# Attention heads of a transformer layer: results normalised in place instead of turned by TensorE, and seven score banks for the last two heads

## The chip, the cores and the metric

The kernel runs on one core of a Trainium2 chip. The metric is the device time of one execution in microseconds (us), the median of several runs. The engines of the core work side by side and wait for each other by semaphores: TensorE (PE; its weight loads are listed as PEld), VectorE (DVE), ScalarE (ACT), GpSimd (POOL) and SyncE (SP), which here issues all the DMAs.

## What is computed

A transformer layer on 4 sequences of 2048 rows of 256: layer norm, self-attention with 16 heads of size 16 and a relative position bias, and a feed-forward part with a router beside it, all added to the input.

```python
def _L0_attn_ref(hidden_states, W_qkv, W_out, rel_emb):      # hidden_states: 4 x 2048 x 256
    qkv = hidden_states @ W_qkv
    ...
    scores = jnp.einsum('bhqd,bhkd->bhqk', q, k)
    scores = scores + compute_bias(rel_emb, S, S)
    attn = jax.nn.softmax(scores.astype(jnp.float32), axis=-1).astype(scores.dtype)
    out = jnp.einsum('bhqk,bhkd->bhqd', attn, v)
    out = jnp.transpose(out, (0, 2, 1, 3)).reshape(B, S, EMBED_DIM)
    return out @ W_out
...
xn = _layernorm(x, axis=-1)
x = x + _L0_attn_ref(xn, ...) + _L0_ffn_ref(xn, ...)
```

## The kernel before

All loops are unrolled, so the order in which instructions are written for each engine is the order in which it takes them. There are three stages.

**Stage 1** (to about 583 us): layer norm, q, k, v, the feed-forward part, the bias, and the row maxima of the first two heads. The change doesn't touch it.

**Stage 2** (to about 3374 us): 64 heads n (4 sequences x 16), each in 16 blocks kb of 128 keys, each block against 2048 queries in four chunks c of 512. For every block TensorE makes four score matmuls (`scores`, L962) into a ring of three PSUM banks, and between them four matmuls for the row maxima of the head two ahead (`maxima`, L946, LEAD = 2) into banks 3 to 6; then the sums of the block two earlier (`sums`, L971, LAG = 2) into bank 7, where the numerators of the head and, in a 17th row of each group of 32, the totals of the softmax gather. ScalarE takes the exponential of each score tile into a buffer prob of four blocks (L832). GpSimd multiplies the parts near the diagonal by the bias factors (L876). VectorE reduces the maxima, two halves a block (L905); TensorE may write the next block's maxima only when it has done so (`wait(pe, max_done, ...)`).

The maxima become the shift of the softmax: at block 8 (TURN_SHIFT) of head n TensorE transposes the maxima of head n+1 (L958), ScalarE copies them to shift_row (L804) and SyncE copies that into a row of the query stack of head n+1 (L775).

The result of head n-1 is finished in head n: at block 2 ScalarE copies bank 7 to o_sb (`collect`, L810); at block 4 (TURN_RESULT) TensorE transposes it with four transposes into a ring bank (L987), ScalarE copies that to o_turned_sb (L816), VectorE takes the reciprocals of the totals (L918), and GpSimd multiplies and writes rows into v_all (`normalise`, L860).

SyncE's order in head n is: load(n+3), the loads of the stacks and bias factors (L144, L770), which wait for head n-1 to be done, then shift(n+1).

**Stage 3** (to the end), 16 chunks of 512 rows: ScalarE packs the results of 16 heads into rows (L1097), TensorE transposes them, ScalarE and VectorE split them in a high and a low part (L1108, L1127), TensorE multiplies by W_out (24 matmuls a chunk, L1171), VectorE adds the base rows (L1139), SyncE stores the chunk and loads base rows for a later one.

Of the kernel before, what the change touches and what calls it, by code (L numbers as in the profile page):

```python
# [14 lines left out]
H, D = 16, 16  # L15
# [28 lines left out]
PROBS = 4  # L44
LAG = 2

# [83 lines left out]
def transformer_layer(nc, x, w_qkv, w_out, rel_emb, router_w, w1, b1, w2, b2, hot, out):  # L130
# [4 lines left out]
    base_d = nc.dram_tensor("base_rows", [B * S, E], F32).ap()  # L135

    def load_stacks(sp, n, q_stack, k_stack, loaded):

        for which, stack, loads in ((0, q_stack, Q_LOADS), (1, k_stack, K_LOADS)):
            for row, part, parts, copies in loads:  # L140
                rows = qk_d[which, part:part + parts, bass.ds(D * n, D), :]
                if copies > 1:
                    rows = rows.to_broadcast([copies, D, S])
                sp.dma_start(stack[D * row:D * (row + parts * copies), :].bitcast(F32), rows).then_inc(loaded, 16)  # L144

    ctx = ExitStack()
    with ctx:
# [21 lines left out]
        with c1:  # L169
# [419 lines left out]
            def _(pe):  # L589
# [22 lines left out]
                def early_scores(b, c, piece):  # L612
# [3 lines left out]
                    for h in range(2):  # L616
                        last = nc.tensor.matmul(ps[:, h], q_early[HALF * h:HALF * h + ROWS, P * i:P * (i + 1)],  # L617
                                                k_early[HALF * h:HALF * h + ROWS, CH * j:CH * (j + 1)], start=True, stop=True)
# [78 lines left out]

        c2 = ExitStack()  # L700
        with c2:
# [3 lines left out]
            ones_row = sb("ones_row", [1, S], F32R, c=c2)  # L705
# [6 lines left out]
            o_sb = sb("o_sb", [P, CH], c=c2)  # L712
            o_turned_sb = sb("o_turned_sb", [P, TPC, CPB, 32], c=c2)
            recip = sb("recip", [P, TPC, CPB], c=c2)

            stacks_in = [sem(f"stacks_in{u}") for u in range(GROUP)]
            shift_in = [sem(f"shift_in{u}") for u in range(GROUP)]
# [3 lines left out]
            v_ones_set = sem("v_ones_set")  # L721
            score_ready = sem("score_ready")
# [6 lines left out]
            shift_turned = sem("shift_turned")  # L729
            o_copied = sem("o_copied")  # L730
            o_turned = sem("o_turned")
            recip_done = sem("recip_done")
            o_done = sem("o_done")

            RING = 3
            MAX_BANK = RING
            SUM_BANK = 7


            TURN_RESULT, TURN_SHIFT = 4, 8  # L740
            RESULT_AT = CPB * TURN_RESULT
            SHIFT_AT = CPB * TURN_SHIFT + 1
            RING_TILES = CPB * KB + 2

            def tile_at(kb, c):

                return CPB * kb + c + (kb >= TURN_RESULT) + (kb >= TURN_SHIFT)

            def drained_at(n, at):


                count = RING_TILES * n + at + 1
                if isinstance(n, int):
                    count += (n == 0 and at < RESULT_AT) - (n == NH - 1 and at >= SHIFT_AT)
                return count
# [8 lines left out]
            def _(sp):  # L764
                def load(n, u):
# [4 lines left out]
                    sp.dma_start(near[u][:], near_d[bass.ds(n % H, 1)].rearrange("a p s c -> (a p) s c")).then_inc(near_in[u], 16)  # L770

                def shift(n, u):

                    wait(sp, drained, 1 if isinstance(n, int) and n == 0 else drained_at(n - 1, SHIFT_AT))
                    sp.dma_start(q_st[u][ROWS:ROWS + 1, :].bitcast(F32).rearrange("a (i p) -> a i p", p=P),  # L775
                                 shift_row[:, n % 2 if isinstance(n, int) else u % 2, :].bitcast(F32)) \
                        .then_inc(shift_in[u], 16)

                def group(g, last=False):
                    for u in range(GROUP):  # L780
                        n = GROUP * g + u
                        if not (last and u > 0):
                            load(n + GROUP - 1, (u + GROUP - 1) % GROUP)
                        if not (last and u == GROUP - 1):
                            shift(n + 1, (u + 1) % GROUP)

                load(0, 0)
                sp.wait_ge(ones_set, 1)
                for u in range(GROUP):
                    sp.dma_start(k_st[u][ROWS:ROWS + 1, :].bitcast(F32), ones_row[:].bitcast(F32)).then_inc(ones_in, 16)  # L790
                shift(0, 0)
                for u in range(1, GROUP - 1):
                    load(u, u)
                group(0)
                for g in range(1, GROUPS - 1):
                    group(g)
                group(GROUPS - 1, last=True)

            @block.scalar
            def _(act):  # L800
                def shift(n, par):

                    wait(act, shift_turned, n + 1)
                    nc.scalar.activation(shift_row[:, par % 2, :], ps[0:KB, SHIFT_AT % RING, 0:P], ACT.Copy).then_inc(drained, 1)  # L804

                def collect(n):

                    wait(act, pv_done, CPB * KB * (n + 1))
                    wait(act, o_turned, n)
                    nc.scalar.activation(o_sb[:], ps[:, SUM_BANK], ACT.Copy).then_inc(o_copied, 1)  # L810

                def collect_turned(n):

                    wait(act, o_turned, n + 1)
                    wait(act, o_done, n)
                    nc.scalar.activation(o_turned_sb[:].rearrange("p i c w -> p (i c w)"), ps[:, RESULT_AT % RING], ACT.Copy) \  # L816
                        .then_inc(drained, 1)

                def head(n, u, first=False, last=False):
                    for kb in range(KB):  # L820
                        if kb == LAG and not first:
                            collect(n - 1)
                        if kb == TURN_RESULT and not first:
                            collect_turned(n - 1)
                        if kb == TURN_SHIFT and not last:
                            shift(n + 1, (u + 1) % GROUP)
                        for c in range(CPB):
                            i = CPB * (KB * n + kb) + c
                            wait(act, score_ready, i + 1)

                            wait(act, pv_done, summed(n, kb - PROBS, c) if kb >= PROBS else summed(n - 1, KB + kb - PROBS, c))
                            nc.scalar.activation(prob[:, kb % PROBS, CH * c:CH * (c + 1)], ps[:, tile_at(kb, c) % RING], ACT.Exp).then_inc(drained, 1)  # L832

                shift(0, 0)
                for u in range(GROUP):
                    head(u, u, first=u == 0)
                for g in range(1, GROUPS - 1):
                    for u in range(GROUP):
                        head(GROUP * g + u, u)
                for u in range(GROUP):  # L840
                    head(NH - GROUP + u, u, last=u == GROUP - 1)
                collect(NH - 1)
                collect_turned(NH - 1)

            @block.gpsimd
            def _(pool):
                def build(n, u, turn):
                    wait(pool, pv_done, CPB * KB * (n - 1))
                    pool.wait_ge(v_ones_set, 2)
                    nc.gpsimd.tensor_copy(vx[:, u % 2, :, 0:D], v_all[:, bass.ds(n, 1)].rearrange("p a k d -> p (a k) d")) \  # L850
                        .then_inc(v_read, 1)

                    pool.wait_ge(near_in[u], 16 * turn)
                    wait(pool, v_read, n + 1)
                    nc.gpsimd.tensor_tensor(vr[:, u % 2], vx[:, u % 2],
                                            near[u][:, 0, 0:1].unsqueeze(2).to_broadcast([P, KB, 32]), ALU.mult).then_inc(v_built, 1)

                def normalise(n):

                    nc.gpsimd.tensor_tensor(  # L860
                        v_all[:, bass.ds(n, 1)].rearrange("p a (c i) d -> p i (a c) d", c=CPB), o_turned_sb[:, :, :, 0:D],
                        recip[:].unsqueeze(3).to_broadcast([P, TPC, CPB, D]), ALU.mult).then_inc(o_done, 1)

                def head(g, u, first=False, last=False):
                    n = GROUP * g + u
                    for kb in range(KB):
                        if kb == TURN_RESULT + 2 and not first:

                            wait(pool, recip_done, n)
                            wait(pool, v_read, n)  # L870
                        if kb == 8 and not last:
                            build(n + 1, (u + 1) % GROUP, g + 1 if u + 1 < GROUP else g + 2)
# [12 lines left out]
                for u in range(GROUP):  # L885
                    head(0, u, first=u == 0)
# [322 lines left out]
```

## Time and profile before

| | |
|---|---|
| median of 3 runs | 3451.89 us (3449.85 to 3497.42) |
| profiled execution | 3448.83 us |
| its span, first to last instruction | 3447.1 us |
| granted TensorE clock, mean | 0.988 of full |
| busy share: PE, DVE, ACT, POOL | 94%, 80%, 72%, 35% |

The profiled execution is one run of the program, 0.1% faster than the median. The span is from the first to the last instruction. A busy share is the time in which an engine works on at least one instruction. In a timeline, each line is an instruction or several like ones: start, duration, engine, line of the kernel, operation, output and inputs, and in brackets the engine's idle time before it with what ended it. Matmuls overlap: each starts before the last has ended. "SPq" is SyncE issuing a DMA; the duration is that of the issue, not of the transfer.

### The profile page before, as it was taken

The numbers are of one execution on the slowest core, as the hardware profiler recorded it, in microseconds if no ns is written. First come the engines' busy times: TensorE is split into PE (matmuls) and PEld (weight loads), VectorE is DVE, ScalarE is ACT, GpSimd is POOL, SyncE is SP. The second block draws the span as 40 slices with busy tenths as digits, with TensorE's granted clock in tenths as the row PEclk, the third lists the DMA queues.
The fourth block names the chain that finished last, engine by engine and source line by source line (L and its number), as shares of the span: only waits on it lengthen the run. The fifth ranks groups of instructions, "written<-read, shape, count | busy, mean of one in ns | idle before, by whom it ended". The sixth has DMA issues, their size and how long they took to land. (4 is left out here: it accounts for less than half of the span.)

```text
span 3447.1 us, 56397 instructions
## 1 busy us (share of the span) xinstructions
PE 3245.1 (94%) x20426; PEld 1573.3 (46%) x20426; DVE 2769.0 (80%) x3046; ACT 2476.0 (72%) x4875; POOL 1203.8 (35%) x1644
## 2 busy tenths in 40 slices
PE   8899997699999999999999999999999999999998
PEld 7788886233333333333333333333333333333337
DVE  5477764588888888888888888888888888888815
ACT  4343443588878887888878888788878887888875
POOL 1112121233433344434444344333443334333430
PEclk9999999799999999999999999999999999999999
DMA  7332323100000000000000000000000000000006
GB/s 183 115 88 74 102 82 101 47 28 28 28 28 28 28 28 28 28 28 28 28 28 28 28 28 28 28 28 28 28 28 28 28 28 28 28 28 28 15 1 199
DMA packets 80480, 156.52 MB, mean 45 GB/s; under 512 B 8088, under 2 KB 48728, under 8 KB 73864
## 3 DMA queue, kind: packets, MB, share of 16 engines
q1 hardware_dynamic: 80200, 152.90, 15.5%
q8 instruction: 161, 2.64, 0.3%
q14 instruction: 119, 0.97, 0.1%
HBM read 101.92 MB, written 56.16 MB: 46 GB/s over the span
## 5 line engine op out<-in xcount | busy, mean ns | idle before, releaser
L905 DVE TENSOR_REDUCE max_half<-ps 128x1 f32<-128x1024 f32 x1984 | 2337.2, 1220 | 337.0 <-PE ps L946 333.6
L832 ACT ACTIVATE prob<-ps 128x512 f32<-128x512 f32 x4096 | 2114.8, 603 | 506.9 <-PE ps L962 506.8
L962 PE MATMUL ps<-q_st,k_st 49*128 49x512 f32 x4096 | 1511.3, 446 | 160.7 <-ACT prob L832 52.5
L946 PE MATMUL ps<-k_st,q_st 48*128 48x512 f32 x3968 | 1569.4, 468 | 0.2 <-DVE max_half L905 0.2
L876 POOL TENSOR_TENSOR prob<-prob,near 128x224 f32<-128x224 f32 (+2 forms) x1408 | 965.1, 691 | 1667.8 <-ACT prob L832 1649.0
L962 PEld LDWEIGHTS ps<-q_st,k_st 49*128 49x128 f32 x4096 | 679.2, 184 | 1334.7 <-ACT prob L832 1142.2
L971 PE MATMUL ps<-prob,vx 128*32 128x512 f32 x4096 | 947.8, 606 | 0.0
L971 PE MATMUL ps<-prob,vr 128*32 128x512 f32 x4096 | 946.1, 604 | 0.0
L946 PEld LDWEIGHTS ps<-k_st,q_st 48*128 48x128 f32 x3968 | 656.3, 184 | 58.7 <-DVE max_half L905 2.5
L608 PE MATMUL ps<-xnt,w_parts 128*128 128x512 f32 x1152 | 276.7, 400 | 16.7 <-DMA k_early<-qk_parts 10.5
L608 PEld LDWEIGHTS ps<-xnt,w_parts 128*128 128x128 f32 x1152 | 218.1, 191 | 70.1 <-DMA k_early<-qk_parts 10.7
L549 ACT ACTIVATE parts<-ps 128x512 fp32r<-128x512 f32 x64 | 38.1, 598 | 272.0 <-PE ps L608 232.6
L971 PEld LDWEIGHTS ps<-prob,vr 128*32 128x32 f32 x4096 | 133.1, 108 | 172.9 <-ACT prob L832 144.9
L673 PE MATMUL ps<-w_parts,hid 128*128 128x256 f32 x1536 | 196.7, 284 | 0.0
L673 PEld LDWEIGHTS ps<-w_parts,hid 128*128 128x128 f32 x1536 | 184.2, 189 | 11.7 <-issue 11.7
L971 PEld LDWEIGHTS ps<-prob,vx 128*32 128x32 f32 x4096 | 132.5, 108 | 78.7 <-ACT prob L832 53.2
L360 POOL TENSOR_TENSOR top_exp<-euler,top_less 128x32 f32<-128x32 f32 x16 | 86.8, 5428 | 160.7 <-DVE top_less L413 160.7
L354 POOL TENSOR_TENSOR rstd<-var_eps,power 128x4 f32<-128x4 f32 x17 | 23.1, 1359 | 307.6 <-DVE var_eps L388 307.6
L557 ACT ACTIVATE hid_raw<-ps,b_sb 128x512 f32<-128x512 f32 x128 | 88.2, 690 | 42.3 <-PE ps L608 32.6
L458 DVE TENSOR_TENSOR parts<-ps,parts 128x512 fp32r<-128x512 f32 x64 | 44.1, 692 | 71.6 <-ACT parts L549 71.6
L475 DVE TENSOR_TENSOR hid<-hid_raw,hid 128x512 fp32r<-128x512 f32 x128 | 85.4, 688 | 19.3 <-ACT hid L564 17.9
L448 DVE TENSOR_REDUCE max_early<-ps 128x2 f32<-128x1024 f32 x64 | 78.4, 1225 | 19.2 <-PE ps L617 18.9
(70 smaller groups left out, 1060.4 us busy)
## 6 DMA issues: line engine op xcount, KB each, us to landing
qk_parts<-parts SPq DMA_DIRECT2D x64, 512.0 KB, 4.6
near<-bias_near SPq DMA_DIRECT2D x64, 352.0 KB, 13.4
q_st<-qk_parts SPq DMA_DIRECT2D x64, 256.0 KB
k_st<-qk_parts SPq DMA_DIRECT2D x64, 256.0 KB
x_sb<-in_L_attn_hidden_states SPq DMA_DIRECT2D x18, 512.0 KB, 6.1
base_rows<-x_sb SPq DMA_DIRECT2D x16, 512.0 KB, 2.9
q_st<-qk_parts SPq DMA_DIRECT2D x64, 128.0 KB
k_st<-qk_parts SPq DMA_DIRECT2D x64, 128.0 KB
```

What stands on the lines that cost most here:

```text
L360: nc.gpsimd.tensor_tensor(top_exp[:], euler[:], top_less[:], ALU.pow).then_inc(exp_done, 1)
L448: nc.vector.tensor_reduce(max_early[:, :, bass.ds(i, 1), j], ps[:, 0:2].unsqueeze(2), AX.X, ALU.max).then_inc(max_done, 1)
L475: nc.vector.tensor_tensor(hid[:, 1, f], hid_raw[:, f % RAWS], hid[:, 0, f].bitcast(F32), ALU.subtract).then_inc(hid_low, 1)
L557: nc.scalar.activation(hid_raw[:, f % RAWS], ps[:, F1_BANKS[f % 4]], ACT.Gelu_apprx_tanh, bias=b1_sb[:, f:f + 1]) \
L608: last = nc.tensor.matmul(to, stationary(a, k), moving(b, k), start=k == 0 and (a, b) == PASSES[0], stop=k == blocks - 1 and (a, b) == PAS ...
L673: last = nc.tensor.matmul(ps[:, F2_BANKS[t % 2], E * (t // 2):E * (t // 2 + 1)], hid[:, a, f, P * t:P * (t + 1)], weight(W_2, b_, f), star ...
L832: nc.scalar.activation(prob[:, kb % PROBS, CH * c:CH * (c + 1)], ps[:, tile_at(kb, c) % RING], ACT.Exp).then_inc(drained, 1)
L876: nc.gpsimd.tensor_tensor(prob[:, kb % PROBS, q0:q1], prob[:, kb % PROBS, q0:q1], near[u][:, side, c0:c0 + q1 - q0], ALU.mult).then_inc(ne ...
L905: nc.vector.reduce_max(max_half[:, par % 2, i, half:half + 1], ps[:, MAX_BANK + 2 * half:MAX_BANK + 2 + 2 * half].rearrange("p a n -> p (a ...
L946: mm = nc.tensor.matmul(ps[:, MAX_BANK + c], q_st[u][0:ROWS, P * i:P * (i + 1)], k_st[u][0:ROWS, CH * c:CH * (c + 1)], start=True, stop=True)
L962: nc.tensor.matmul(ps[:, tile_at(kb, c) % RING], k_st[u][:, P * kb:P * (kb + 1)], q_st[u][:, CH * c:CH * (c + 1)], start=True, stop=True). ...
L971: nc.tensor.matmul(ps[32 * c:32 * (c + 1), SUM_BANK], v[:, u % 2, kb], prob[:, kb % PROBS, CH * c:CH * (c + 1)], start=kb == 0, stop=kb == ...
```

## The change

- The result of a head is no longer turned. It stays in o_sb (now two buffers), transposed as bank 7 has it. SyncE copies the totals from it to total_sb by four DMAs (`totals`), VectorE takes the reciprocals (`reciprocals`, after block TOTAL_AT = 6), SyncE stores them to DRAM and spreads them over recip_rows by four broadcasts (`spread`), GpSimd multiplies o_sb in place (`normalise`, after block NORM_AT = 10), and SyncE copies the result by four DMAs into attn (`keep`), which lies in a new buffer for the first sequence and in v_all for the others. In each head this comes behind shift(n+1) in SyncE's order.
- The shift is turned by TensorE as before, at block TURN_AT = 8.
- prob has three blocks, not four.
- Heads 62 and 63, which have no maxima to make, use seven banks for scores: from tile ALONE on.
- The last stage joins the same block. attn is transposed already, so nothing is packed or turned: ScalarE makes the high part of a chunk (`high`, 128x1024), GpSimd the low part (`low`, 128x1024), TensorE multiplies, VectorE adds. Two chunks are prepared ahead of the last head's end, the others behind it. W_out and the first base rows are loaded in head 1.

```diff
-PROBS = 4
+PROBS = 3
 LAG = 2
+TURNED = 3
...
+            TOTAL_AT, NORM_AT, TURN_AT = 6, 10, 8
+            def tile_at(n, kb, c):
+                return CPB * (KB * n + kb) + c + n + 1 + (kb >= TURN_AT and n < NH - 1)
+            def turn_at(m):
+                return CPB * (KB * (m - 1) + TURN_AT) + m if m > 0 else 0
+            ALONE = tile_at(NH - LEAD, 0, 0)
+            def bank_of(at):
+                return at % RING if at < ALONE else (at - ALONE) % SUM_BANK
...
             @block.sync
+                def shift(n):
+                    wait(sp, drained, turn_at(n) + 1)
+                    sp.dma_start(q_st[n % GROUP][ROWS:ROWS + 1, :]..., shift_row[:, n % 2].bitcast(F32)).then_inc(shift_in[n % GROUP], 16)
+                def totals(n):
+                    sp.wait_ge(o_copied, n + 1)
+                    wait(sp, recip_done, n)
+                    for c in range(CPB):
+                        sp.dma_start(total_sb[32 * c:32 * (c + 1)], o_sb[32 * c + D:32 * c + D + 1, n % 2].rearrange("a (g i) -> a g i", i=PIECE)) \
+                            .then_inc(total_in, 16)
+                def spread(n):
+                    sp.wait_ge(recip_done, n + 1)
+                    sp.dma_start(recip_d[n].rearrange("(p i) -> p i", i=PIECE), recip[:]).then_inc(recip_stored, 16)
+                    sp.wait_ge(recip_stored, 16 * (n + 1))
+                    wait(sp, o_done, n)
...
+                    for c in range(CPB):
+                        sp.dma_start(recip_rows[32 * c:32 * c + D], recip_d[n:n + 1, CH * c:CH * (c + 1)].to_broadcast([D, CH])).then_inc(recip_in, 16)
+                def keep(n):
+                    sp.wait_ge(o_done, n + 1)
...
+                for n in range(NH):
+                    if n + GROUP - 1 < NH:
+                        load(n + GROUP - 1)
+                    if n + 1 < NH:
+                        shift(n + 1)
+                    if n > 0:
+                        totals(n - 1)
+                        spread(n - 1)
+                        keep(n - 1)
...
             @block.scalar
+                for i in range(TURNED - 1):
+                    high(i)
+                collect(NH - 1)
+                for i in range(TURNED - 1, B * CPB):
+                    high(i)
             @block.gpsimd
+                def normalise(n):
+                    pool.wait_ge(recip_in, 16 * CPB * (n + 1))
+                    nc.gpsimd.tensor_tensor(o_sb[:, n % 2], o_sb[:, n % 2], recip_rows[:], ALU.mult).then_inc(o_done, 1)
...
+                for i in range(TURNED - 1):
+                    low(i)
+                normalise(NH - 1)
+                for i in range(TURNED - 1, B * CPB):
+                    low(i)
             @block.vector
+                def reciprocals(n):
+                    dve.wait_ge(total_in, 16 * CPB * (n + 1))
+                    wait(dve, recip_stored, 16 * n)
+                    nc.vector.reciprocal(recip[:], total_sb[:]).then_inc(recip_done, 1)
...
+                for n in range(NH):
+                    for kb in range(KB):
+                        if n + LEAD < NH:
+                            maxima(n + LEAD, kb)
+                        if kb == TOTAL_AT and n > 0:
+                            reciprocals(n - 1)
+                    if n + LEAD < NH:
+                        combine(n + LEAD, max_half)
...
             @block.tensor
-                def turn_result(n):
-                    wait(pe, o_copied, n + 1)
-                    for i in range(TPC):
-                        last = nc.tensor.transpose(ps[:, RESULT_AT % RING, P * i:P * (i + 1)], o_sb[:, P * i:P * (i + 1)], ident[:])
-                    last.then_inc(o_turned, 1)
...
+                        if kb == TURN_AT and n + 1 < NH:
+                            turn(n + 1)
+                        for c in range(CPB):
+                            scores(n, kb, c)
+                            if m < NH:
+                                maxima(m, kb, c)
```

## Rows read from the trace of the kernel before

**Rows 1.** The page's costliest groups: busy, mean ns of one, idle before
```profile
L905 DVE TENSOR_REDUCE max_half<-ps 128x1 f32<-128x1024 f32 x1984 | 2337.2, 1220 | 337.0 <-PE ps L946 333.6
...
L962 PEld LDWEIGHTS ps<-q_st,k_st 49*128 49x128 f32 x4096 | 679.2, 184 | 1334.7 <-ACT prob L832 1142.2
```
**Rows 2.** Timeline of one undisturbed block: start us, duration us, engine
```profile
2028.43 0.50 PE L962 MATMUL ps<-q_st,k_st 49*128 49x512 f32 x1
...
2029.23 2.35 DVE L905 TENSOR_REDUCE max_half<-ps 128x1 f32<-128x1024 f32 x2 [0.26 <-PE ps L946]
...
2029.61 0.50 PE L962 MATMUL ps<-q_st,k_st 49*128 49x512 f32 x1
...
2031.04 0.50 PE L962 MATMUL ps<-q_st,k_st 49*128 49x512 f32 x1
```
**Rows 3.** Timeline around block 8, where the shift is turned
```profile
2021.19 2.36 DVE L905 TENSOR_REDUCE max_half<-ps 128x1 f32<-128x1024 f32 x2 [0.26 <-PE ps L946]
...
2023.21 0.49 PE L962 MATMUL ps<-q_st,k_st 49*128 49x512 f32 x1
...
2023.59 1.04 POOL L855 TENSOR_TENSOR vr<-vx,near 128x512 f32<-128x512 f32 x1
2023.61 0.56 SPq L775 DMA_DIRECT2D q_st<-shift_row  x1
...
2025.82 0.49 PE L962 MATMUL ps<-q_st,k_st 49*128 49x512 f32 x1
```
**Rows 4.** Timeline of SyncE's issues, and DMA issues: KB each, us to landing
```profile
2000.41 1.09 SPq L144 DMA_DIRECT2D q_st<-qk_parts  x2
2001.54 1.17 SPq L144 DMA_DIRECT2D k_st<-qk_parts  x2
...
q_st<-shift_row SPq DMA_DIRECT2D x64, 8.0 KB, 1.8
...
k_st<-ones_row SPq DMA_DIRECT2D x4, 8.0 KB, 3.0
```
**Rows 5.** Timeline around block 4, where the result is turned
```profile
2009.30 0.50 PE L962 MATMUL ps<-q_st,k_st 49*128 49x512 f32 x1
...
2012.50 0.50 PE L962 MATMUL ps<-q_st,k_st 49*128 49x512 f32 x1
...
2015.57 0.24 DVE L918 RECIPROCAL recip<-o_turned_sb 128x16 f32<-128x16 f32 x1
```
**Rows 6.** Stretches: us, busy (instructions) per engine, PEclk, DMA share, GB/s
```profile
583.00:584.00 1.00, 0.10 (x1) 0.00 (x0) 0.96 (x3) 0.00 (x0) 0.00 (x0) 1.00 0.00 0
...
587.00:588.00 1.00, 0.04 (x1) 0.04 (x1) 0.32 (x2) 0.00 (x0) 0.36 (x1) 0.79 0.00 0
...
642.00:643.00 1.00, 1.00 (x10) 0.25 (x10) 1.00 (x2) 1.00 (x3) 0.84 (x2) 0.90 0.15 42
```
**Rows 7.** Timeline of the first head, TensorE at the low clock
```profile
634.90 2.36 DVE L905 TENSOR_REDUCE max_half<-ps 128x1 f32<-128x1024 f32 x2 [0.18 <-PE ps L946]
...
637.32 0.79 PE L946 MATMUL ps<-k_st,q_st 48*128 48x512 f32 x1
...
640.33 0.79 PE L962 MATMUL ps<-q_st,k_st 49*128 49x512 f32 x1
...
643.40 0.50 PE L962 MATMUL ps<-q_st,k_st 49*128 49x512 f32 x1
```
**Rows 8.** Timeline of two blocks of the last head, without maxima
```profile
3355.84 0.96 PE L962 MATMUL ps<-q_st,k_st 49*128 49x512 f32 x3
...
3358.44 0.96 PE L962 MATMUL ps<-q_st,k_st 49*128 49x512 f32 x3
```
**Rows 9.** The last stage: timeline, and one stretch of it
```profile
3373.37 0.60 ACT L810 ACTIVATE o_sb<-ps 128x512 f32<-128x512 f32 x1 [1.94 <-PE ps L971]
...
3392.31 3.11 PE L1171 MATMUL ps<-wo_parts,turned 128*128 128x256 f32 x24
...
3412.00:3416.00 4.00, 4.00 (x36) 4.00 (x35) 2.92 (x7) 2.56 (x7) 0.00 (x0) 1.00 0.88 283
```

More of the change, by code:

```diff
@@ L769, in load @@
                     wait(sp, near_done, NEAR_UP_TO[KB] * (n - GROUP + 1))
[L770 to L787, printed above, removed]
+                    sp.dma_start(near[u][:], near_d[n % H:n % H + 1].rearrange("a p s c -> (a p) s c")).then_inc(near_in[u], 16)
@@ L791, in _ @@
[L791 to L826, printed above, removed]
-                        for c in range(CPB):
[L828 to L843, printed above, removed]
@@ L1072, in batch @@
+                totals(NH - 1)
+                spread(NH - 1)
+                keep(NH - 1)
+                for b in range(B):
                     for c in range(CPB):
-                        wait(sp, res_done, TPC * (CPB * b + c + 1))
-                        sp.dma_start(out[bass.ds(S * b + CH * c, CH), :].rearrange("(t p) e -> p t e", p=P), base_in[:, c]) \
+                        sp.wait_ge(res_done, TPC * (CPB * b + c + 1))
+                        sp.dma_start(out[S * b + CH * c:S * b + CH * (c + 1), :].rearrange("(t p) e -> p t e", p=P), base_in[:, c]) \
@@ new lines, in collect, with head @@
+                def collect(n):
+                    act.wait_ge(pv_done, CPB * KB * (n + 1))
+                    if n > 1:
+                        act.wait_ge(attn_in[(n - 2) // H], 16 * CPB * ((n - 2) % H + 1))
+                    nc.scalar.activation(o_sb[:, n % 2], ps[:, SUM_BANK], ACT.Copy).then_inc(o_copied, 1)
+                def head(n):
+                    for kb in range(KB):
+                        if kb == LAG and n > 0:
+                            collect(n - 1)
+                        if kb == TURN_AT and n + 1 < NH:
+                            shift(n + 1)
+                        for c in range(CPB):
+                            act.wait_ge(score_ready, CPB * (KB * n + kb) + c + 1)
+                            t = KB * n + kb
+                            if t >= PROBS:
+                                act.wait_ge(pv_done, summed((t - PROBS) // KB, (t - PROBS) % KB, c))
+                            nc.scalar.activation(prob[:, t % PROBS, CH * c:CH * (c + 1)], ps[:, bank_of(tile_at(n, kb, c))], ACT.Exp) \
+                                .then_inc(drained, 1)
@@ new lines, in high @@
+                def high(i):
+                    b, c = i // CPB, i % CPB
+                    act.wait_ge(attn_in[b], 16 * CPB * H)
+                    wait(act, proj_ready, TPC * (i - TURNED + 1))
+                    nc.scalar.activation(turned[:, i % TURNED, 0], attn[b][:, :, CH * c:CH * (c + 1)], ACT.Copy).then_inc(a_high, 1)
+                shift(0)
+                for n in range(NH):
+                    head(n)
+                    if n == 2:
+                        act.wait_ge(wo_in, 16)
+                        nc.scalar.activation(wo_parts[:, 0], wo_raw, ACT.Copy).then_inc(wo_high, 1)
@@ L1142, in _, with maxima @@
-                dve.wait_ge(wo_high, 1)
-                nc.vector.tensor_tensor(wo_parts[:, 1], wo_raw[:], wo_parts[:, 0].bitcast(F32), ALU.subtract).then_inc(wo_low, 1)
-                low(0, 0)
-                batch(0)
-                for b in range(1, B - 1):
-                    batch(b)
-                batch(B - 1)
+                def maxima(m, i):
+                    for half in range(2):
+                        dve.wait_ge(max_ready, 2 * (KB * m + i) + half + 1)
+                        if i == 0 and half == 0:
+                            wait(dve, neg_done, m - 1)
+                        nc.vector.reduce_max(max_half[:, m % 2, i, half:half + 1],
+                                             ps[:, MAX_BANK + 2 * half:MAX_BANK + 2 + 2 * half].rearrange("p a n -> p (a n)"), AX.X).then_inc(max_done, 1)
@@ new lines, in sums @@
+                def sums(n, kb):
+                    if kb == 0:
+                        pe.wait_ge(v_built, n + 1)
+                        wait(pe, o_copied, n)
+                    for c in sum_order(kb):
+                        if near_at(kb, c):
+                            pe.wait_ge(near_done, NEAR_UP_TO[KB] * n + near_at(kb, c))
+                        else:
+                            pe.wait_ge(drained, tile_at(n, kb, c) + 1)
+                        v = vr if c < left_chunks(kb) else vx
+                        nc.tensor.matmul(ps[32 * c:32 * (c + 1), SUM_BANK], v[:, n % 2, kb], prob[:, (KB * n + kb) % PROBS, CH * c:CH * (c + 1)],
+                                         start=kb == 0, stop=kb == KB - 1).then_inc(pv_done, 1)
@@ L1156, in turn @@
+                for kb in range(KB - LAG, KB):
+                    sums(NH - 1, kb)
+                pe.wait_ge(wo_low, 1)
+                pe.wait_ge(drained, tile_at(NH - 1, KB - 1, CPB - 1) + 1)
+                for i in range(B * CPB):
+                    pe.wait_ge(a_low, i + 1)
                     for t in range(TPC):
+                        wait(pe, res_done, TPC * (i - 1) + t + 1)
                         for k in range(KE):
-                            last = nc.tensor.transpose(ps[:, TURN_BANKS[c % 2] + k, P * t:P * (t + 1)], rows[:, c % 2, t, P * k:P * (k + 1)],
-                                                       ident[:])
@@ L1178, in _ @@
-                turn(0, 0)
-                turn(1, 1)
-                pe.wait_ge(wo_low, 1)
-                batch(0)
-                for b in range(1, B - 1):
-                    batch(b)
-                batch(B - 1)
+                            for x, y in PASSES:
+                                last = nc.tensor.matmul(ps[:, PROJ_BANK + t, 0:E], turned[:, i % TURNED, x, k, P * t:P * (t + 1)], wo_parts[:, y, k],
+                                                        start=k == 0 and (x, y) == PASSES[0], stop=k == KE - 1 and (x, y) == PASSES[-1])
```

424 lines of the change are left out of this document (156 added, 268 removed).

## The prediction

> **What bounds the kernel now.** I read the table of stretches first, then the costliest groups, then the timeline of single heads. From about 631 to 3373 us the kernel does one thing 64 times: a head of 16 key blocks (kb), 42.8 us each. No engine is full there. The costliest group on VectorE is the row maxima for the head two ahead, 1984 of 1220 ns each; the weight loads of the scores spend most of their idle time behind an exponential [rows 1]. The timeline of one block shows why [rows 2]: the first score starts at 2028.43, the fourth, which needs the ring bank that the first exponential frees, at 2029.61, and the first score of the next block at 2031.04. A block lasts 2.61 us, in this relay between TensorE and ScalarE. VectorE is nearly level with it: its two maxima of the block take 2.35 of those 2.61 us, starting 0.80 us after the first score. So VectorE has 0.26 us of slack a block. TensorE may not write the maxima of block kb+1 before VectorE has read those of block kb (the wait on max_done in maxima). **An instruction that holds VectorE for more than a fraction of a microsecond holds TensorE, and with it everything.** This is what the change has to be read against.
>
> **Part 1: result rows no longer turned.** Before, TensorE turns the summed head at block 4 by four transposes. The block before it, from 2009.30 to the first score behind the transposes at 2012.50, takes 3.20 us in place of 2.61 [rows 2, 5]: 0.59 us, on the path. It goes in heads 1 to 63: 63 x 0.59 = 37 us gained. ScalarE's copy of the turned result goes too; it lay in the wait behind those transposes. The shift's transpose at block 8 stays.
>
> **Part 2: the totals go round by DMA, and where that puts VectorE's wait.** The new order of waits, read from the diff, is this. In head n, VectorE does the maxima of blocks 0 to 6 and then `reciprocals(n-1)` (TOTAL_AT = 6), which waits for `total_in`. The four copies that raise it are issued by SyncE in `totals(n-1)`. SyncE issues them only behind `shift(n+1)`, and that waits for ScalarE's copy of the shift, which TensorE's transpose at block 8 (TURN_AT = 8) releases. So a wait placed after block 6 is satisfied by something that cannot start before block 8. It is no deadlock: TensorE gets through block 7, whose maxima need only those of block 6 read, does the transpose and the first score of block 8, and then stands at the first maximum of block 8, which needs half of block 7's maxima read. Behind it on TensorE stand the other scores and the sums, behind these ScalarE's exponentials and GpSimd's products.
>
> Its size, with t = 0 at the first score of block 8 (2023.21 in the kernel before) [rows 3]. SyncE issues the shift at +0.40. Issues of this kind follow one another by (2001.54 - 2000.41)/2 = 0.57 us [rows 4], so the fourth totals copy starts at 0.40 + 4 x 0.575 = 2.70. The nearest copy by kind and size, shift_row, lands 1.8 us after its issue [rows 4]: 4.50. The reciprocal takes 0.25 [rows 5]: 4.8 with the hand-over. Then two maxima of 1.18 each (half of 2.35) [rows 2]: 5.98 and 7.16. TensorE follows about 0.06 us behind (634.90 + 2.36 = 637.26, and the matmul at 637.32) [rows 7]: at 7.22 it writes the third maximum of block 8. Undisturbed, block 9 would have begun at 2.61.
>
> Meanwhile TensorE has been idle from about 0.5 to 6.0. Does the clock fall? After its last matmul at 583.1 it was granted 1.00 until within the second 587 to 588, where the mean is 0.79, so it fell 4.7 us after it [rows 6]. I take it that 5.5 us of idling is enough: the head goes on at 1.2 GHz and not at 2.4. The cost is in the first head of before, where the loop starts at the low level under the same wait on VectorE [rows 7]: from the matmul at 637.32 (the same third maximum) to the first score of the next block at 640.33 are 3.01 us, and that block, in which the clock rises (0.90 in 642 to 643 [rows 6]), takes 3.07 to 643.40. So block 9 begins at 7.22 + 3.01 = 10.23 and block 10 at 13.30, in place of 5.22. **The delay is 8.1 us a head.** VectorE loses nothing more after that; its halves then end before TensorE asks.
>
> The wait bites where VectorE still has maxima to do, and where there is a head before: n from 1 to 61. 61 x 8.1 = 494 us.
>
> Bounds of this term. If the clock held, the third maximum at 7.22 would be followed by the fourth score at 7.46 and 1.43 us of sums (2029.61 to 2031.04) [rows 2], block 10 would begin at 11.5, and the delay would be 6.3 us: 384 us. If the copies landed like the ones_row copies, at 3.0 [rows 4], it would be 9.3: 567 us. If the clock rose a block later, that block would take about 3.95 (its first-to-fourth score 1.45, then as the 3.01 less the pair, an estimate from [rows 7]) and not 3.07: 9.0, or 549 us. Both together give 10.2.
>
> The skill has a rule against this change here. The Trainium skill, DMA: Bandwidth & Descriptors (Specifications), says that pieces under 512 B are done by read-modify-write, and these copies write 64 B pieces; its section on why small descriptors are slow confines the penalty to HBM, and these go from SBUF to SBUF. By the first the sum would move towards the 3.0 us landing, by the second stay at 1.8. No row of before has pieces of 64 B.
>
> **Part 3: the rest of that round trip.** After the reciprocal SyncE stores it, waits, and issues four broadcasts: 4.8 + 3.0 (landing bound) + 3 x 0.575 + 3.0 puts `recip_in` at about 12.5 after t = 0, while GpSimd asks for it only after the products of block 10, that is after 13.3 + 2. Nothing waits. GpSimd's multiplication, 128x512, costs 1.04 as the nearest such operation does [rows 3]; it lies in GpSimd's idle time. `keep` and its four copies follow at about 17 to 20, long before ScalarE reuses the buffer two heads later, and SyncE is back in time for the loads at the next head. Cover gone: only head 62, whose blocks are short and have no stall. There `recip_in` comes at 12.5, GpSimd's products of block 11 end at about 14.5, and the sums that need them would start at about 12.4: 1 to 2 us once. Taken: +1. Three prob buffers for four cost nothing, since an exponential of kb waits for sums that TensorE has in any case issued before that score.
>
> **Part 4: seven score banks in heads 62 and 63.** Without maxima a block still takes 2.60 us (3355.84 to 3358.44) [rows 8]: the fourth score waits for its ring bank 1.18 us after the first, with three issued. With seven banks it can follow at about 0.81 (three take 0.96 including the last one's tail, pitch 0.24), which saves 0.37 a block: 32 x 0.37 = 12 us. Below lies nothing, above the pace of four exponentials, 17 us.
>
> **Part 5: the output projection.** From the last sums, just before 3373.37 [rows 9], to the end of the span there are 73.7 us before. The new stage needs no packing and no transposes, so a chunk costs TensorE 3.1 us, 24 matmuls [rows 9], not 3.74, and it begins about 1.4 us after the last sums instead of 10. But GpSimd's third chunk stands behind `normalise(63)`, which waits for the last head's round trip: copy of the sums until +0.9, four totals issues and landing (4.5), reciprocal (4.8), store (7.3 to 7.8), four broadcasts (11.5 to 12.5), multiplication. It starts at about 12.6 and ends at 14.8 (two inputs of 128x1024, twice 1.04 [rows 3]). SyncE's first output store waits as long, until 15. From there 16 stores and 12 loads of 0.52 MB, 14.7 MB, at the 283 GB/s of before [rows 9], take 52 us, TensorE's 14 chunks 14 x 3.1 = 43 us. The stores decide: 15 + 52 = 67, less a little for reads that overlap better: 66. So 8 us gained, within -2 and +12.
>
> **Sum**, against the profiled execution (span 3447.1, time 3448.8, which is 3 us or 0.1% under the median of the runs, 3451.9): 3447.1 - 37 + 494 + 1 - 12 - 8 = 3885, and 1.7 around the span: **3887 us**, 12.6% more than the median.
>
> **The rivals.**
> *The clock holds* (chance 0.12). For it: 5.5 us of idling is only just above the 4.7 us after which it fell. Against it: in the only such gap shown it did fall. 3887 - 110 = 3777 us. The Trainium skill, TensorE: Matmul & The Clock Gate (HAM oscillation), describes a loop whose bursts are parted by DMA waits and which restarts at the low level every time; by that this rival falls away and the 494 stands.
> *The copies or the issue are slower, or the clock stays down longer* (0.23). For it: 64 B pieces, and the 3.0 us landing. Against it: the same queue is empty then. 3942 to 3960, both together near 4010.
> *The stall isn't there: VectorE's wait is satisfied in time* (0.05), which ends on the other side. Its place is VectorE after block 6, whose maxima end at -2.61 + 0.80 + 2.35 - 2.61 = -2.07 on the scale above; total_in would have to be there by then, since the idle 0.26 us just hold a reciprocal of 0.25. What would remain is 3448.8 - 37 - 12 - 8 = 3392 us, 1.7% less than the median. For it speaks only that o_copied is set at block 2, six blocks earlier; against it SyncE's order in the diff, shift ahead of totals.
> *The forecast* has 0.60, and 3840 to 3935 as its own range.
>
> Range: 3775 to 3985, from the held clock to slow copies or a late clock; about 0.12 is left out on both sides. A measurement of this kernel tells about 2% from no change. All cases but the third are slower by more than that: slower 0.95, within 2% 0.04, faster 0.01.
>
> **What would show it.** In the profile after: VectorE's reciprocals with an idle time of 5 to 7 us before each of 61 of them, ended by a DMA into total_sb; the maxima matmuls of block 8 released by VectorE; a period of about 50 us a head up to head 61; a granted clock that falls to 1.2 GHz once in every head, with a mean near 0.9 of full over the heads; blocks of 2.2 us in the last two heads; a gap of some 5 us in TensorE after two chunks of the projection. It is wrong if VectorE's reciprocals come without a wait, if the period is 42, or if the gap is in another place (ScalarE waiting for shift_in or attn_in, GpSimd for recip_in).

## The result and the profile after

The changed kernel takes 3945.26 us (median; 3939.31 to 3988.68), the kernel before 3450.87 in the same comparison: 1.142 times as long, interval 1.130 to 1.155. The prediction was 3887 us in a range of 3775 to 3985. The profiled execution of after spans 3948.1 us. Its four executions differ by 49 us, and the longer ones have the lower clock: spans of 3937.5, 3938.8, 3948.1 and 3986.9 us at a mean granted clock of 0.910, 0.909, 0.906 and 0.885.

| | before | after |
|---|---|---|
| span of the profiled execution, us | 3447.1 | 3948.1 |
| granted TensorE clock, mean | 0.988 | 0.906 |
| one head in the middle, us | 42.8 | 51.2 |
| one block in the last two heads, us | 2.60 | 2.11 |
| from the last head's copy of the sums to the end, us | 73.7 | 63.1 |

The page of after, costliest groups. The columns are as in [rows 1]: busy, mean ns of one, then the engine's idle time before the group and what ended most of it.

```profile
L989 DVE TENSOR_REDUCE max_half<-ps 128x1 f32<-128x1024 f32 x1984 | 2333.1, 1218 | 439.3 <-PE ps L1033 437.1
L1033 PE MATMUL ps<-k_st,q_st 48*128 48x512 f32 x3968 | 1659.6, 500 | 343.7 <-DVE max_half L989 343.6
...
L1002 DVE RECIPROCAL recip<-total_sb 128x16 f32<-128x16 f32 x64 | 16.2, 253 | 502.0 <-DMA total_sb<-o_sb 502.0
```

The third line holds the cause: 64 reciprocals that are busy for 16 us, with VectorE idle for 502 us before them, all of it ended by the copies into total_sb. Of these, 428 us lie before the reciprocals of heads 1 to 61, 7.0 us each. The other 74 us lie before the last three, when VectorE has no maxima left to do, and hold nobody up. The second line is the echo one engine further: TensorE stood 344 us before maxima matmuls, released by VectorE. In the kernel before, the same group waits 0.2 us:

```profile
L946 PE MATMUL ps<-k_st,q_st 48*128 48x512 f32 x3968 | 1569.4, 468 | 0.2 <-DVE max_half L905 0.2
```

One of these waits in the timeline of after (start, duration; the shift's issue is L805, the totals' copies L813, the reciprocal L1002; compare [rows 3]):

```profile
2038.54 2.36 DVE L989 TENSOR_REDUCE max_half<-ps 128x1 f32<-128x1024 f32 x2 [0.25 <-PE ps L1033]
...
2043.16 0.50 PE L1044 MATMUL ps<-q_st,k_st 49*128 49x512 f32 x1
...
2043.56 0.56 SPq L805 DMA_DIRECT2D q_st<-shift_row  x1
...
2044.23 2.44 SPq L813 DMA_DIRECT2D total_sb<-o_sb  x4
2047.89 0.25 DVE L1002 RECIPROCAL recip<-total_sb 128x16 f32<-128x16 f32 x1 [7.00 <-DMA total_sb<-o_sb]
2048.06 2.29 DVE L989 TENSOR_REDUCE max_half<-ps 128x1 f32<-128x1024 f32 x2
...
2049.28 0.79 PE L1033 MATMUL ps<-k_st,q_st 48*128 48x512 f32 x1 [5.62 <-DVE max_half L989]
...
2053.42 0.79 PE L1044 MATMUL ps<-q_st,k_st 49*128 49x512 f32 x1
...
2057.31 0.49 PE L1044 MATMUL ps<-q_st,k_st 49*128 49x512 f32 x1
```

With t = 0 at 2043.16, the first score of block 8: shift issued at +0.40, the two maxima after the reciprocal done at 7.19, block 9 at 10.26, block 10 at 14.15. The prediction had 0.40, 7.16, 10.23 and 13.30. And the clock over the same stretch, one microsecond each (busy time and number of instructions of PE, PEld, DVE, ACT, POOL, then the granted clock, DMA share, GB/s):

```profile
2045.00:2046.00 1.00, 0.00 (x0) 0.00 (x0) 0.00 (x0) 0.00 (x0) 0.00 (x0) 1.00 0.03 3
2046.00:2047.00 1.00, 0.00 (x0) 0.00 (x0) 0.00 (x0) 0.00 (x0) 0.00 (x0) 0.92 0.05 4
2047.00:2048.00 1.00, 0.00 (x0) 0.00 (x0) 0.11 (x1) 0.00 (x0) 0.00 (x0) 0.50 0.03 2
...
2056.00:2057.00 1.00, 1.00 (x8) 0.00 (x0) 1.00 (x1) 0.33 (x1) 0.83 (x1) 0.50 0.00 0
2057.00:2058.00 1.00, 1.00 (x10) 0.49 (x6) 0.07 (x1) 0.16 (x1) 0.00 (x0) 0.96 0.00 0
```

TensorE's last matmul before the wait ends at 2043.66. The clock falls to 1.2 GHz 3.2 us later, at 2046.8, and comes back at 2057.1, when TensorE has been at work again for 7.8 us.

### The profile page after: what moved, and what is told of

It is laid out like the page before. It is cut to its first block, busy times and chain, and to the rows that moved or that the text cites. A ratio compares the mean times of both kernels' runs of the same rounds, so it can differ in the third digit from the quotient of the medians.

```text
span 3948.1 us, 56312 instructions
## 1 busy us (share of the span) xinstructions
PE 3416.9 (87%) x20042; PEld 1591.0 (40%) x20042; DVE 2746.3 (70%) x3014; ACT 2437.0 (62%) x4731; POOL 1281.2 (32%) x1661
## 4 chain that ended last, share of the span: by engine, by line
PE 58%; ACT 14%; DMA 4%; SPq 4%; issue 3%; DVE 2%; POOL 0%; ACTq 0%; DVEq 0%
PE ps L1064 29%; PE ps L1044 25%; ACT prob L908 13%; PE ps L1033 4%; DMA total_sb<-o_sb 3%; SPq L813 3%; DVE max_half L989 2%; SPq L805 1%; DMA k_st<-qk_parts 1%; PE ps L1100 1%; DMA out_rows<-base_in 0%; ACT shift_row L886 0%; DVE recip L1002 0%; PE ps L1050 0%; SPq L146 0%
## 5 line engine op out<-in xcount | busy, mean ns | idle before, releaser
L1033 PE MATMUL ps<-k_st,q_st 48*128 48x512 f32 x3968 | 1659.6, 500 | 343.7 <-DVE max_half L989 343.6
L1044 PE MATMUL ps<-q_st,k_st 49*128 49x512 f32 x4096 | 1603.9, 477 | 142.0 <-DMA k_st<-qk_parts 43.0
L1044 PEld LDWEIGHTS ps<-q_st,k_st 49*128 49x128 f32 x4096 | 731.1, 199 | 1423.4 <-ACT prob L908 1057.2
L1064 PE MATMUL ps<-prob,vr 128*32 128x512 f32 x4096 | 1058.1, 662 | 0.0
L1064 PE MATMUL ps<-prob,vx 128*32 128x512 f32 x4096 | 1058.1, 662 | 0.0
L1033 PEld LDWEIGHTS ps<-k_st,q_st 48*128 48x128 f32 x3968 | 710.3, 201 | 459.1 <-DVE max_half L989 404.5
L1002 DVE RECIPROCAL recip<-total_sb 128x16 f32<-128x16 f32 x64 | 16.2, 253 | 502.0 <-DMA total_sb<-o_sb 502.0
L481 DVE TENSOR_TENSOR hid<-hid_raw,hid 128x512 fp32r<-128x512 f32 x128 | 85.4, 688 | 19.3 <-ACT hid L570 17.9
```

Of the source, the lines that this page charges most:

```text
L481: nc.vector.tensor_tensor(hid[:, 1, f], hid_raw[:, f % RAWS], hid[:, 0, f].bitcast(F32), ALU.subtract).then_inc(hid_low, 1)
L1033: mm = nc.tensor.matmul(ps[:, MAX_BANK + c], query_block(q_st[u][0:ROWS], i), k_st[u][0:ROWS, CH * c:CH * (c + 1)], start=True, stop=True)
L1044: nc.tensor.matmul(ps[:, bank_of(at)], k_st[u][:, P * kb:P * (kb + 1)], q_st[u][:, CH * c:CH * (c + 1)], start=True, stop=True).then_inc(s ...
L1064: nc.tensor.matmul(ps[32 * c:32 * (c + 1), SUM_BANK], v[:, n % 2, kb], prob[:, (KB * n + kb) % PROBS, CH * c:CH * (c + 1)], start=kb == 0, ...
```

## The experiments

Two theories stand against each other. **The order**: VectorE's wait after block 6 is for copies that SyncE issues behind the shift of block 8. **The round trip**: what the change added (nine small DMAs beside the four of `keep`, GpSimd's multiplication, one prob buffer fewer) costs the time wherever it stands. Inside the first, a second question: how much of a head's 9.1 us is the wait and how much the clock.

### The totals' copies ahead of the shift

```diff
+                    if n > 0:
+                        totals(n - 1)
                     if n + 1 < NH:
                         shift(n + 1)
                     if n > 0:
-                        totals(n - 1)
                         spread(n - 1)
```

> The changed kernel with one line moved: SyncE issues the four totals copies of head n-1 ahead of the shift of head n+1; every DMA, multiplication and buffer stays. If the order is the cause (VectorE's wait after block 6 for copies that stand behind a shift of block 8), the reciprocals come without a wait, a head takes 42.1 us and not 51.2, the clock stays at 2.4 GHz, and the time is about 3945 - 61 x 9.1 - 14 = 3376 us (the 14 are four heads that lost 3.4 us more). If it is the round trip itself, its DMAs, GpSimd's multiplication or the three prob buffers, the time stays near 3900.

Measured: 3384.76 us (3382.94 to 3387.34), ratio to the kernel before 0.981, interval 0.980 to 0.983. A head takes 42.1 us. The timeline of VectorE in this kernel:

```profile
2043.13 2.36 DVE L990 TENSOR_REDUCE max_half<-ps 128x1 f32<-128x1024 f32 x2 [0.25 <-PE ps L1034]
2045.40 0.24 DVE L1003 RECIPROCAL recip<-total_sb 128x16 f32<-128x16 f32 x1
2045.74 2.36 DVE L990 TENSOR_REDUCE max_half<-ps 128x1 f32<-128x1024 f32 x2
```

The reciprocal slips in between two maxima with no wait. With the same DMAs, the same multiplication and three prob buffers an undisturbed block still takes 2.61 us, so they cost nothing that shows; 560 us hung on one position in SyncE's list. The theory of the round trip is out.

### The wait later instead of the copies earlier

```diff
-            TOTAL_AT, NORM_AT, TURN_AT = 6, 10, 8
+            TOTAL_AT, NORM_AT, TURN_AT = 10, 14, 8
```

> The changed kernel with SyncE's order as it is, but VectorE's reciprocals after block 10 and GpSimd's normalisation after block 14. By the theory of the order the copies land 4.5 us after block 8 begins, before VectorE asks at about 8.4, so this gives the same as moving the copies: about 3376 us, with GpSimd perhaps waiting a little for the broadcasts. If the copies disturb by being issued in the middle of the head, it stays well above 3450.

Measured: 3387.47 us (one run), 42.1 to 42.3 us a head. SyncE's order is the faulty one here, and it does no harm. Neither the copies' position nor the wait's is bad by itself; what counts is which comes first in time.

### The wait one and two blocks later

```diff
-            TOTAL_AT, NORM_AT, TURN_AT = 6, 10, 8
+            TOTAL_AT, NORM_AT, TURN_AT = 7, 10, 8
```

> The changed kernel with VectorE's reciprocals one block later, after block 7. The same wait ends at the same moment, but TensorE then gets one block further: its third maximum of block 9 comes at about 7.2 us after the start of block 8 and not at 3.2, a delay of 3.7 us with the clock held, and TensorE idles 2.9 us and not 5.6. Clock held: 3376 + 61 x 3.7 = 3602 us. Clock lost as before (2.8 us a head): 3770 us.

```diff
-            TOTAL_AT, NORM_AT, TURN_AT = 6, 10, 8
+            TOTAL_AT, NORM_AT, TURN_AT = 8, 10, 8
```

> The changed kernel with VectorE's reciprocals after block 8. The wait then reaches TensorE in block 10: delay 1.1 to 1.7 us a head, idle time of TensorE under 2 us, so the clock is held: 3376 + 61 x 1.5 = 3467 us. If any such wait costs the clock: 3640 us.

Measured: 3825.35 and 3517.41 us (one run each), both more than expected for a held clock (3602 and 3467). The first is 55 us above even the number for a lost clock, 3770; the second stays under its 3640. After block 7, a head takes 48.5 or 50.5 us, in turns over most of the run; after block 8, 43.1 to 43.4 in 37 of 61 heads (1.1 more than 42.1, as expected for a held clock) and 43.5 to 50.4 in the others. The wait is as short as worked out. In the kernel with the wait after block 7 TensorE stands 2.99 us, from timeline and stretches:

```profile
2032.03 0.25 DVE L1002 RECIPROCAL recip<-total_sb 128x16 f32<-128x16 f32 x1 [4.38 <-DMA total_sb<-o_sb]
...
2033.41 0.50 PE L1033 MATMUL ps<-k_st,q_st 48*128 48x512 f32 x1 [2.99 <-DVE max_half L989]
...
2034.54 0.79 PE L1033 MATMUL ps<-k_st,q_st 48*128 48x512 f32 x1 [0.39 <-DVE max_half L989]
```

```profile
2033.00:2034.00 1.00, 0.59 (x4) 0.30 (x4) 1.00 (x2) 0.04 (x1) 0.00 (x0) 1.00 0.09 8
2034.00:2035.00 1.00, 0.61 (x4) 0.46 (x3) 1.00 (x2) 1.00 (x2) 0.00 (x0) 0.67 0.11 33
2041.00:2042.00 1.00, 1.00 (x9) 0.49 (x6) 0.19 (x1) 0.04 (x1) 1.00 (x1) 0.92 0.00 0
```

The first matmul after the gap still runs in 0.50 us; the clock falls 0.9 us later, with TensorE already at work, and stays down until 2041.2. So a wait that TensorE has behind it can still cost the clock, and here it did in each of the 61 heads. That is why the number for the held clock failed: a head has 3.7 us of delay, as expected, and another 2.7 (42.1 + 3.7 + 2.7 = 48.5), about the 2.8 taken for a lost clock. In the heads of 50.5 us it is 4.7, since the clock stays down longer, and that neither number had. With the wait after block 8 the clock fell in 22 of the 61 heads. In nine of these TensorE had gaps of at most 0.42 us before the fall, in the others up to 1.6, while most heads with gaps of 0.4 us kept the clock.

### TensorE kept at work during the wait

```diff
                             scores(n, kb, c)
+                            if kb == TURN_AT and c == 0 and n > 0 and m < NH:
+                                wait(pe, drained, before_in_bank(tile_at(n, kb, 1)) + 1)
+                                for _ in range(44):
+                                    nc.tensor.transpose(ps[:, bank_of(tile_at(n, kb, 1)), 0:P], ident[:], ident[:])
                             if m < NH:
```

> The changed kernel with 44 transposes of the identity matrix put into TensorE's wait at block 8 of heads 1 to 61, into a free score bank, about 5.2 us of otherwise idle time; they are overwritten by the next score and change nothing in the result. The wait for VectorE stays as long. If 2.8 of the 9.1 us a head are the clock, the stretch behind the wait now runs at 2.4 GHz, a head takes 48.4 us and the time is about 3945 - 61 x 2.8 - 14 = 3760 us. If the delay is the wait alone, it stays at 3945 or grows.

Measured: 3802.6 us (one run). In most heads VectorE waits as long as before, and TensorE resumes its maxima 1.1 us after the reciprocal's end, as before, but at 2.4 GHz. One of these heads:

```profile
2128.37 0.25 DVE L1002 RECIPROCAL recip<-total_sb 128x16 f32<-128x16 f32 x1 [6.97 <-DMA total_sb<-o_sb]
...
2129.76 0.50 PE L1033 MATMUL ps<-k_st,q_st 48*128 48x512 f32 x1 [0.65 <-DVE max_half L989]
```

```profile
2128.00:2129.00 1.00, 1.00 (x11) 0.87 (x8) 0.63 (x2) 0.00 (x0) 0.00 (x0) 1.00 0.00 0
2129.00:2130.00 1.00, 0.35 (x4) 0.24 (x4) 1.00 (x2) 0.00 (x0) 0.00 (x0) 1.00 0.09 8
```

41 of the 61 heads take 48.4 to 48.7 us, which is 42.1 + 6.3: the bound that the prediction had worked out for a held clock. The other 20 take 49 to 55. In 19 of them the copies land later than usual, so that VectorE waits 7.2 to 8.8 us, and in eight of these the clock falls all the same; that is why the run took 3803 us and not 3760. So of the 9.1 us a head, 6.3 are the wait and 2.8 the clock.

### One copy of the totals in place of four

```diff
-                    for c in range(CPB):
-                        sp.dma_start(total_sb[32 * c:32 * (c + 1)], o_sb[32 * c + D:32 * c + D + 1, n % 2].rearrange("a (g i) -> a g i", i=PIECE)) \
-                            .then_inc(total_in, 16)
+                    sp.dma_start(total_sb[:], o_sb[D:P:32, n % 2].rearrange("a (g i) -> a g i", i=PIECE)).then_inc(total_in, 16)
...
-                    dve.wait_ge(total_in, 16 * CPB * (n + 1))
+                    dve.wait_ge(total_in, 16 * (n + 1))
```

> The changed kernel with the totals of the four row groups brought by one DMA and not four. The wait ends three issues earlier, 3 x 0.6 = 1.8 us. If the issues are a term of the stall one for one and the clock still falls (3.8 us of idling): 3945 - 61 x 1.8 = 3835 us. If the clock then holds: 3945 - 110 - 171 - 14 = 3650 us. If the landing depends on the slowest piece and not on the issues: about 3945.

Measured: 3868.66 us (one run), 77 less than the changed kernel and not 110. The timeline of this kernel:

```profile
2005.25 0.56 SPq L805 DMA_DIRECT2D q_st<-shift_row  x1
2005.92 0.61 SPq L812 DMA_DIRECT2D total_sb<-o_sb  x1
```

```profile
2007.91 0.25 DVE L1000 RECIPROCAL recip<-total_sb 128x16 f32<-128x16 f32 x1 [5.33 <-DMA total_sb<-o_sb]
```

From the issue of the shift to the reciprocal are 2.66 us, with four copies 4.33: 1.67 less, close to the 1.8 expected, so the issues are a term of the wait. But a head got only 77 / 61 = 1.3 us shorter on the mean: the periods are now 48.3 to 52.8, since the clock stays down for more than 13 us in 16 of the 61 heads (for less than 7 in ten), in the profile of the changed kernel in four (mean granted clock 0.88 from 2000 to 3000 us, there 0.90). A part of the shorter wait is given back there.

### Three banks in the last two heads

```diff
             def bank_of(at):
 
-                return at % RING if at < ALONE else (at - ALONE) % SUM_BANK
+                return at % RING
```

> The kernel with the totals copies ahead of the shift, but with three score banks in the last two heads too. Blocks there go back from 2.11 to 2.60 us: 32 x 0.49 = 16 us more than with seven banks, about 3392 us. If ScalarE or GpSimd set the pace there anyway, no difference.

This is made on the kernel with the totals ahead. Measured: 3400.26 us (one run), 15.5 more than that one: the seven banks are worth what the blocks show, 32 x 0.49.

### The last stage in another order

```diff
-                keep(NH - 1)
                 for b in range(B):
                     for c in range(CPB):
+                        if (b, c) == (0, 2):
+                            keep(NH - 1)
...
-                for i in range(TURNED - 1):
+                for i in range(TURNED + 1):
                     low(i)
                 normalise(NH - 1)
-                for i in range(TURNED - 1, B * CPB):
+                for i in range(TURNED + 1, B * CPB):
                     low(i)
```

> The kernel with the totals copies ahead of the shift, and the last stage put in another order: GpSimd makes the low parts of chunks 2 and 3 before the last head's normalisation, SyncE stores chunks 0 and 1 before it copies the last head's result. TensorE's gap of 5.6 us after chunk 1 closes and the stores begin some 7 us earlier. Since 14.7 MB at about 320 GB/s are 46 us and lie behind the first store: 5 to 7 us less than without, about 3370 us. If the last stores are bound by something else, the same as without.

Also made on the kernel with the totals ahead, and the fastest of all: 3378.78 us (3376.72 to 3381.23), ratio to the kernel before 0.978, interval 0.975 to 0.982, 6.0 us less than without. The gap in TensorE closes. The kernel without this edit, then with it:

```profile
3332.63 2.72 PE L1101 MATMUL ps<-wo_parts,turned 128*128 128x256 f32 x11 [5.71 <-POOL turned L965]
3332.78 1.14 SPq L873 DMA_DIRECT2D out_rows<-base_in  x2
```

```profile
3323.36 14.99 PE L1102 MATMUL ps<-wo_parts,turned 128*128 128x256 f32 x120 [0.18 <-DVE base_in L1026]
...
3326.74 0.97 SPq L874 DMA_DIRECT2D out_rows<-base_in  x2
```

The stores begin 8.3 us after the last copy of the sums (3318.44), not 13.9 (3318.90), and the end comes 5.9 us earlier (57.8 for 63.8 us). The edit closes the gap and brings the stores forward together, so by itself it does not show which of the two decides. The chain of work that ended last tells more. From 3330 us on it runs, without the edit, through TensorE's projection matmuls for 49% of the time and through the transfers of result and base rows for 35%; with it, the transfers have 77%. So the stores decide the whole stage only once the gap is closed.

## Why the prediction was right, and where a term was off

Against the profiled span of 3447.1 us:

| term | predicted | measured | by |
|---|---|---|---|
| result rows not turned, 63 heads | -37 | -42 | heads of 42.79 and 42.13 us; 2 us in head 62 |
| the wait in 61 heads | +494 | +567 | heads 1 to 61: 3137.4 us, with the totals ahead 2570.2 |
| GpSimd in head 62 | +1 | +0.6 | a block of 2.69 for 2.11 us |
| seven banks | -12 | -15.5 | the kernel with three |
| last stage | -8 | -10.6 | 63.1 for 73.7 us |
| a later first score, not in the prediction | | +2.0 | 633.1 for 631.1 us |
| sum | 3885 | 3948.6 | span 3948.1 |

**The reading of the order was right**, and with it the sign and the place: VectorE's wait, then TensorE at the first maximum of block 8, released by VectorE, in heads 1 to 61. TensorE's gap behind two chunks of the projection came too, 5.6 us. The rival that the copies come in time is refuted by the 61 waits of 7.0 us, and its own sum, 3392, was close to what the kernel with the totals ahead takes, 3385.

**The path through the wait was right to 0.1 us at its end**: block 9 begins at 10.26 after t = 0, predicted 10.23. On the way the copies landed 0.2 us later than worked out (reciprocal at 4.73, predicted 4.50), and shorter hand-overs made up for it. The landing of the copies is 1.8 us, as for shift_row in [rows 4]; pieces of 64 B cost nothing more here. The section on small descriptors in the Trainium skill's page DMA: Bandwidth & Descriptors, which limits the penalty to HBM, agrees with this; the read-modify-write of its Specifications does not show in the landing. With the totals ahead of the shift, the same copies land in 2.3 us in the median.

**Mis-sized: the term for block 9, 3.07 us.** It was taken from the one block of before in which the clock rose [rows 6, 7], where the rise came 4.9 us after the third maximum (642.2 and 637.32). In after it comes 6.7 us after it (2057.1 and 2050.41), so block 9 runs at the low level almost to its end, 2053.42 to 2057.31: 3.89 us. That is the shortest of the 61; the median is 4.04. With it the delay is 10.24 + 4.04 - 5.22 = 9.1 us, which is the "clock rose a block later" bound of the prediction, 3.95 and 9.0 us a head, that I had put among the rivals. It is the ordinary case: 56 heads take 51.1 to 51.3 us and head 61 51.8. Four heads, in a row, take 54.5 to 55.1, since the clock stays down longer still. Their first, from the stretches of after:

```profile
1828.00:1830.00 2.00, 0.00 (x0) 0.00 (x0) 0.22 (x2) 0.00 (x0) 0.00 (x0) 0.59 0.04 3
...
1844.00:1848.00 4.00, 4.00 (x18) 1.31 (x16) 2.36 (x2) 2.08 (x4) 1.01 (x3) 0.50 0.14 33
1850.00:1852.00 2.00, 2.00 (x16) 0.85 (x8) 1.94 (x3) 1.46 (x4) 1.04 (x2) 1.00 0.00 0
```

Low from 1828 to about 1849, with TensorE back at work for the last 17.7 us of it. The two together are the 73 us by which this term fell short; the smaller terms bring that to the 63 by which the profiled span exceeds the 3885 of the sum, and the forecast falls 58 short of the median. The rival with the held clock was wrong for the reason given: the clock did fall in the wait. Its margin had been misread, though: a mean of 0.79 in the second 587 to 588 puts the fall at 587.6, 4.5 us after the last matmul and not 4.7, and in after it came after 3.0 to 3.5.

**The smaller terms** were a little timid. The transposes cost 0.66 a head, not 0.59 (the block behind them was longer too, which I left out). A block with seven banks takes 2.11 us, and ScalarE is busy for 4.91 of the 5 us from 3860 to 3865, so it sets the pace there; I had TensorE at 2.23. That number did not follow from its own pitch either: a fourth score at 3 x 0.24 = 0.72 and not 0.81 would have saved 0.46 a block, 15 us. In head 62 GpSimd waited 2.60 us for recip_rows, but TensorE lost only 0.6 by it. The store of the reciprocals landed in 1.4 us and the broadcasts in 1.8, where I had taken 3.0 as a bound, so everything behind them was early. In the last stage the first store came 13.8 us after the copy of the sums, predicted 15, and the rest took 49.3 us for 52. The stores did not decide all of it: the chain that ended last goes through TensorE's matmuls from 3898.6 to 3918.4 and only then through the transfers.

What stays open: why the first score comes at 631.1 us in the one profile of before and at 632.5 to 635.2 in the nine others, and why the clock comes back after some 8 us of work in 57 heads and after nearly 18 in four.

## What to carry to other kernels

When a result is sent round by DMA, write down for the engine that waits which instruction of which block releases each step, along the issuing queue too: an entry ahead of it in the queue that waits for a later block keeps the wait from ending before that block, though nothing deadlocks. Look for it where two engines are level, as the maxima's reader and TensorE are here with 0.26 us of slack a block. Moving the entry or the wait cost nothing here (3385 and 3387 us). And count the slow clock behind a gap in TensorE beside the gap itself: here it was 2.8 us on 6.3.

## What the runs showed of the hardware

- Clock: in the changed kernel it falls 3.0 to 3.5 us after TensorE's last matmul, in the idle stretch before the first head of before it fell after 4.5. TensorE loses the high level not only in a gap: after a gap of 2.99 us the fall came 0.9 us after work had resumed (wait after block 7), and in nine heads of the kernel with the wait after block 8 it came with gaps of at most 0.42 us, where most heads with such gaps kept the clock (mean 0.966 over that run). A low stretch lasted 3.4 to 20.5 us. Behind a wait, the clock came back after 7.8 to 8.2 us of work in 57 heads of the changed kernel, after 17.7 to 17.9 in four, and after 11.1 in the first head of before. The Trainium skill's page TensorE: Matmul & The Clock Gate (HAM oscillation) describes a loop that falls back in every round; the changed kernel is one, with a fall in each of the heads 1 to 61.
- Shortening a wait can give part of the gain back: 1.67 us less of waiting brought about 1.3 a head (one copy of the totals).
- SyncE issues the totals' copies one every 0.61 us (2.44 for four), the broadcasts from DRAM one every 0.43 (1.71 for four).
- GpSimd multiplies two full 128x512 operands in 1.28 us, where the product with a column broadcast over the row took 1.04 [rows 3]; the subtraction of two of 128x1024 takes 2.36 to 2.40.
